# Spiking feed-forward layer: first layer over gathered w1 rows, and an idle add moved ahead of the second batch's tokens

## What is computed

```python
def _L0_cond_ref(inputs, initial_state):          # x (2, 2048, 512), cond (2, 512)
    rates = jax.nn.relu(inputs) * DT              # DT = 0.001
    c = initial_state[:, None, :] + jnp.cumsum(rates, axis=1)
    fl = jnp.floor(c)
    prev = jnp.concatenate([jnp.floor(initial_state)[:, None, :], fl[:, :-1, :]], axis=1)
    return (fl - prev) / DT

def _L0_ffn_ref(x, w1, b1, w2, b2):               # w1 (512, 2048), w2 (2048, 512)
    h = jax.nn.relu(jnp.einsum('bsd,dw->bsw', x, w1) + b1)
    return jnp.einsum('bsw,wd->bsd', h, w2) + b2

x = x + _L0_ffn_ref(_L0_cond_ref(x, cond), w1, b1, w2, b2)
```

## Time and profile before

| | |
|---|---|
| three runs | 108.17, 106.98, 107.22 us; median 107.22 |
| the profiled execution | 108.13 us, of which the span is 106.4 |
| busy in the span | TensorE 94.6 us (89%), VectorE 67.9, ScalarE 36.2, GpSimd 36.6 |
| data moved | 31.66 MB, mean 298 GB/s |
| mean granted clock of TensorE | 0.98 |

### The profile page before, as it was taken

One profiled execution on the slowest core, in us unless ns is written; L12 is line 12 of the kernel. 1 busy time (PEld: TensorE's weight loads), 2 busy tenths in 40 slices (PEclk: granted clock), 3 DMA queues, 4 the chain that ended last, 5 costly groups with the idle time before them and its releaser, 6 DMA issues.

```text
span 106.4 us, 1159 instructions
## 1 busy us (share of the span) xinstructions
PE 94.6 (89%) x375; PEld 52.2 (49%) x375; DVE 67.9 (64%) x137; ACT 36.2 (34%) x66; POOL 36.6 (34%) x41
## 2 busy tenths in 40 slices
PE   5999999999999999999895999999999999995000
PEld 5844444444644444634251444599999644441000
DVE  2348999888599999385445599999998700022000
ACT  2867515514382353189740000059443200000000
POOL 6200000000077500038300199960018780088720
PEclk9999999999999999999999999999999999999965
DMA  2999999999999999999992000499999999947850
GB/s 90 276 351 407 421 419 411 405 410 411 407 408 408 395 391 413 398 390 386 374 367 91 0 0 6 197 441 397 434 404 397 391 202 354 242 93 99 103 108 9
DMA packets 10028, 31.66 MB, mean 298 GB/s; under 512 B 1671, under 2 KB 1799, under 8 KB 8994
## 3 DMA queue, kind: packets, MB, share of 16 engines
q1 hardware_dynamic: 8304, 29.63, 72.4%
q0 software_dynamic: 1568, 1.90, 10.9%
q10 hardware_dynamic: 146, 0.01, 0.1%
HBM read 21.58 MB, written 10.75 MB: 304 GB/s over the span
## 4 chain that ended last, share of the span: by engine, by line
PE 43%; DVE 15%; POOL 13%; issue 12%; DMA 10%; POOLq 2%; DVEq 0%
PE ps_table L833 37%; DVE x_sb L697 8%; POOL out L357 8%; DMA rates<-in_x_turned,sixteen_at 5%; DMA out<-x_sb 5%; DVE spk_t L638 4%; PE ps_small L934 4%; POOL rates L352 3%; PE ps_turn L870 2%; POOLq L55 2%; POOL out L387 1%; POOL general_x L376 1%; DVE under L579 1%; DVE blocks_under L582 1%; POOLq L267 0%
## 5 line engine op out<-in xcount | busy, mean ns | idle before, releaser
L833 PE MATMUL ps_table<-w_sb 128*128 128x512 f32 x128 | 57.5, 602 | 0.1
L833 PEld LDWEIGHTS ps_table<-w_sb 128*128 128x128 f32 x128 | 24.0, 193 | 27.0 <-issue 26.2
L352 POOL DMA_INDIRECT rates<-in_x_turned,sixteen_at x8 | 9.6, 1198 | 36.9 <-DVE sixteen_at L583 35.0
L428 ACT ACTIVATE w_sb<-w_sb,b_col 128x512 f32<-128x512 f32 (+2 forms) x19 | 12.2, 642 | 16.7 <-DMA w_sb<-in_w_pairs 16.7
L357 POOL DMA_INDIRECT out<-w_sb,to_single x8 | 12.5, 1561 | 15.7 <-DMA out<-x_sb 13.8
L569 DVE SCALAR_TENSOR_TENSOR total_two<-x_sb,total_two 128x1024 f32<-128x1024 f32 x14 | 17.1, 1224 | 1.1 <-DMA x_sb<-in_x 0.6
L929 PE MATMUL ps_table<-w_sb 128*128 128x512 f32 x32 | 14.0, 595 | 0.0
L697 DVE TENSOR_TENSOR x_sb<-x_sb,ps_idle 128x2048 f32<-128x2048 f32 x6 | 13.4, 2277 | 0.1
L364 POOL TENSOR_TENSOR x_sb<-x_sb,idle_row 128x512 f32<-128x512 f32 x8 | 10.1, 1289 | 9.1 <-DVEq L738 9.1
L429 ACT ACTIVATE w_sb<-w_sb,minus_relu_b 128x512 f32<-128x512 f32 (+2 forms) x19 | 12.3, 649 | 0.6
L929 PEld LDWEIGHTS ps_table<-w_sb 128*128 128x128 f32 x32 | 6.0, 190 | 7.2 <-issue 6.9
(11 more groups left out here) (124 smaller groups left out, 54.2 us busy)
## 6 DMA issues: line engine op xcount, KB each, us to landing
x_sb<-in_x SPq DMA_DIRECT2D x16, 512.0 KB, 14.3
out<-x_sb SPq DMA_DIRECT2D x8, 1024.0 KB, 4.8
w_sb<-in_w_pairs SPq DMA_DIRECT2D x15, 512.0 KB, 15.5
w_sb<-in_w SPq DMA_DIRECT2D x4, 1024.0 KB, 16.0
w_sb<-in_w_pairs SPq DMA_DIRECT2D x2, 256.0 KB, 3.1
b_row<-in_b SPq DMA_DIRECT2D x1, 256.0 KB, 15.6
rates<-in_x_turned,sixteen_at POOLq DMA_INDIRECT x8, 5.9
out<-w_sb,to_single POOLq DMA_INDIRECT x8, 6.6
```

The costliest lines, as they stand in the source:

```text
L352: pool.indirect_dma_start(out=rates[:, col, :], out_offset=None, in_=x_sixteen, in_offset=bass.IndirectOffsetOnAxis(ap=sixteen_at[:, col:c ...
L428: chain(act.activation(weights, weights, ACT.Relu, bias=b1_col[:, m:m + 1], scale=PER_DT))
L833: last = pe.matmul(ps_table[c][:, :], table_hidden[:, m, c * P:(c + 1) * P], w2_sb[:, m, :], start=(m == 0), stop=(m == FC - 1))
```

## The change

The first layer of the general tokens no longer multiplies all 512 channels of `spk_t`. Each batch numbers its channels that have a slot (its members), at most 128: `count_members` and `place_members` give each member a place, a product with `place_hot` (`sum_places`) puts the members' channel, slot and row into places, `list_places` turns them into indices, and GpSimd gathers w1's rows for the places (`get_w1`, one indirect DMA of up to 128 rows of 8 KB for a batch). The first layer then is two products of 128 places by 128 slots for a chunk (`general_first`), and it alternates with the second layer (`general_second`). The four loads of `w1_sb` are gone from SyncE's queue (one is left in the redo branch).

The order changes with it. VectorE: `add_idle(0, 0, 4)` stands behind `place_members(0)` and ahead of `find_tokens(1)`; `list_general` stands ahead of the other idle adds; `list_singles` stands ahead of the fourth. TensorE: the new small products stand between parts of the table, `sum_rows` (now two products) between chunks 14 and 15, and the first layer waits for `general_listed` and both gathers. GpSimd: the two w1 gathers, then a wait for `general_listed` and the gather of `general_x`, then the two idle pieces; the wait for `adding` is gone. ScalarE copies the table's rows one step earlier. Memory for flags and facts, the numbering checks and two small conversions at the start change too; they are cut below.

```diff
-            for i in range(WQ):
-                part = slice(i * (F // WQ), (i + 1) * (F // WQ))
-                sp.dma_start(w1_sb[:, :, part], w1.rearrange("(c p) f -> p c f", p=P)[:, :, part]).then_inc(w1_in[i], 16)
...
-            for b in range(B):
+            def get_sixteens(b):
...
+            def get_w1(b):
+                pool.wait_ge(places_listed, b + 1)
+                pool.indirect_dma_start(out=w1_got_rows[b], out_offset=None, in_=w1,
+                                        in_offset=bass.IndirectOffsetOnAxis(ap=w1_at[b][:, :], axis=0)
+                                        ).then_inc(w1_got[b], 16)
...
+            get_sixteens(0)
+            get_sixteens(1)
+            get_w1(0)
             pool.wait_ge(idle_copied, 1)
-            pool.wait_ge(adding, 1)
+            get_w1(1)
+            pool.wait_ge(general_listed, 1)
+            pool.indirect_dma_start(out=general_x[:, :], out_offset=None, in_=x_rows,
+                                    in_offset=bass.IndirectOffsetOnAxis(ap=from_general[:, :], axis=0)
+                                    ).then_inc(general_got, 16)
             add_idle(1, 12, 16)
             add_idle(1, 8, 12)
             pool.wait_ge(singles_listed, 1)
             for b in range(B):
-                if b == 1:
-                    pool.wait_ge(general_listed, 1)
-                    pool.indirect_dma_start(out=general_x[:, :], out_offset=None, in_=x_rows,
-                                            in_offset=bass.IndirectOffsetOnAxis(ap=from_general[:, :], axis=0)
-                                            ).then_inc(general_got, 16)
...
+            act.wait_ge(table_summed, FC)
+            act.activation(table_row[0], ps_table[0][:, :], ACT.Copy).then_inc(table_rows_ready, 1)
             for m in range(FC):
                 relu_hidden(m, hidden_summed, m + 1, hidden_ready)
-                if 1 <= m <= DC:
-                    act.activation(table_row[m - 1], ps_table[m - 1][:, :], ACT.Copy).then_inc(table_rows_ready, 1)
+                if 1 <= m < DC:
+                    act.activation(table_row[m], ps_table[m][:, :], ACT.Copy).then_inc(table_rows_ready, 1)
...
+                chain(dve.tensor_scalar(facts_high[:, own(b), 2:3].rearrange("p e o -> p (e o)"), blocks_under[:, own(b)],
+                                        float(BLK), float(b * S), ALU.mult, ALU.add))
...
-                chain(dve.tensor_reduce(slot[:, mine], slot_part[:, :, :], AXIS.X, ALU.add))
-
-            def first_spikes():
-                chain(dve.tensor_tensor(spk_t[:, :, :], over(slot[:, own(0)], P), along(slot_name, DC), ALU.is_equal))
-
-            def second_spikes():
-                for c in range(DC):
-                    last = dve.scalar_tensor_tensor(out=spk_t[:, c, :], in0=slot_name, scalar=slot[:, DC + c:DC + c + 1],
-                                                    in1=spk_t[:, c, :], op0=ALU.is_equal, op1=ALU.add)
-                    if c < DC - 1:
...
-                last.then_inc(spk_ready, 1)
+                with nc.allow_low_precision(reason="whole numbers that the type holds"):
+                    chain(dve.tensor_reduce(facts_high[:, mine, 1:2].rearrange("p e o -> p (e o)"), slot_part[:, :, :],
+                                            AXIS.X, ALU.add))
+
+            def count_members(b):
+
+                mine = own(b)
+                chain(dve.tensor_scalar(is_member[:, mine], facts_high[:, mine, 1:2].rearrange("p e o -> p (e o)"), 0.5, None,
+                                        ALU.is_gt))
+                chain(dve.tensor_tensor_scan(member_run[b][:, :], ones[:, 0:DC], is_member[:, mine], 0.0, ALU.mult, ALU.add))
+                dve.sem_inc(members_counted, 1)
+                with nc.allow_low_precision(reason="whole numbers that the type holds"):
+                    chain(dve.tensor_reduce(facts_low[:, mine, 2:3].rearrange("p e o -> p (e o)"),
+                                            token_under[:, mine, 1:BLK], AXIS.X, ALU.add))
+
+            def place_members(b):
+                mine = own(b)
+                dve.wait_ge(members_before, b + 1)
+                chain(dve.scalar_tensor_tensor(out=place[:, mine], in0=member_run[b][:, :], scalar=ps_members[b],
+                                               in1=is_member[:, mine], op0=ALU.add, op1=ALU.mult))
+                chain(dve.tensor_tensor(place_hot[b][:, :, :], over(place[:, mine], P), along(slot_name, DC), ALU.is_equal))
+                dve.sem_inc(places_ready, 1)
+
+            def list_places(b):
+                dve.wait_ge(places_summed, b + 1)
+                dve.tensor_copy(w1_at[b][:, :], ps_places[b][:, 0:1]).then_inc(places_listed, 1)
+                dve.tensor_copy(place_fact[b][:, 1:2], ps_places[b][:, 2:3])
+                dve.tensor_scalar(place_slot[b][:, :], slot_name, ps_places[b][:, 1:2], None, ALU.is_equal).then_inc(
+                    slots_placed, 1)
...
-                chain(dve.tensor_reduce(tokens_under[:, :], token_under[:, :, 1:BLK], AXIS.X, ALU.add))
-                chain(dve.scalar_tensor_tensor(out=row_at[:, :], in0=blocks_under[:, :], scalar=float(BLK),
-                                               in1=tokens_under[:, :], op0=ALU.mult, op1=ALU.add))
+                chain(dve.tensor_tensor(row_at[:, :], facts_high[:, :, 2:3].rearrange("p e o -> p (e o)"),
+                                        facts_low[:, :, 2:3].rearrange("p e o -> p (e o)"), ALU.add))
                 chain(dve.tensor_scalar(not_single[:, :], met[:, :], 1.0, FAR, ALU.not_equal, ALU.mult))
...
+                for b in range(B):
+                    chain(dve.tensor_copy(checks[:, b + 1:b + 2], member_run[b][:, DC - 1:DC]))
...
-                chain(dve.tensor_scalar(slot_place[:, :], ps_rows[:, 1:3], slot_count[:, 0:1], None, ALU.mult))
+                chain(dve.tensor_scalar(slot_row[:, :], ps_rows[:, 1:2], slot_count[:, 0:1], None, ALU.mult))
                 chain(dve.tensor_scalar(none_far[:, :], ps_rows[:, 0:1], 0.5, FAR, ALU.is_lt, ALU.mult))
-                chain(dve.scalar_tensor_tensor(out=slot_row[:, :], in0=slot_place[:, 0:1], scalar=float(BLK),
-                                               in1=slot_place[:, 1:2], op0=ALU.mult, op1=ALU.add))
...
             find_sums(1)
             number_general(0)
             find_slots(0)
-            first_spikes()
+            count_members(0)
+            place_members(0)
+            add_idle(0, 0, 4)
             find_tokens(1)
+            list_places(0)
             find_general(1)
             number_general(1)
             find_slots(1)
-            second_spikes()
-            dve.sem_inc(adding, 1)
-            add_idle(0, 0, 4)
+            count_members(1)
+            place_members(1)
+            list_places(1)
+            list_general()
             add_idle(0, 4, 8)
             add_idle(0, 8, 12)
+            list_singles()
             add_idle(0, 12, 16)
-            list_singles()
-            find_members()
-            add_idle(1, 0, 4)
             find_odd()
             count_crowd()
-            list_general()
+            add_idle(1, 0, 4)
             add_idle(1, 4, 8)
...
+            def count_members(b):
+                pe.wait_ge(members_counted, b + 1)
+                pe.wait_ge(sums_ready, B)
+                pe.matmul(ps_members[b], upper_b[:, :], member_run[b][:, DC - 1:DC], start=True, stop=True).then_inc(
+                    members_before, 1)
+
+            def sum_places(b):
+                pe.wait_ge(places_ready, b + 1)
+                for facts in (facts_high, facts_low):
+                    for c in range(DC):
+                        last = pe.matmul(ps_places[b], place_hot[b][:, c, :], facts[:, b * DC + c, :],
+                                         start=(facts is facts_high and c == 0), stop=(facts is facts_low and c == DC - 1))
+                last.then_inc(places_summed, 1)
+
             def sum_rows():
-                pe.wait_ge(members_ready, 1)
-                for e in range(NE):
-                    last = pe.matmul(ps_rows, member[e // DC][:, e % DC, :], facts[:, e, :], start=(e == 0), stop=(e == NE - 1))
+                pe.wait_ge(slots_placed, B)
+                for b in range(B):
+                    last = pe.matmul(ps_rows, place_slot[b][:, :], place_fact[b][:, :], start=(b == 0), stop=(b == B - 1))
                 last.then_inc(rows_summed, 1)
+
+            def general_first(m):
+                if m >= 2:
+                    pe.wait_ge(hidden_ready, m - 1)
+                for b in range(B):
+                    last = pe.matmul(ps_hidden[m % 2][:, 0:P], w1_got_rows[b][:, m * P:(m + 1) * P], place_slot[b][:, :],
+                                     start=(b == 0), stop=(b == B - 1))
+                last.then_inc(hidden_summed, 1)
+
+            def general_second(m):
+                if m == 0:
+                    pe.wait_ge(table_rows_ready, 1)
+                pe.wait_ge(hidden_ready, m + 1)
```

(38 more changed lines are left out.)

68 lines of the change are left out of this document (37 added, 31 removed).

## The result

The changed kernel takes 115.22 us (114.21 to 115.37, four runs) against 107.55 in the runs beside it: 1.069 times as long, 95% interval 1.062 to 1.077. The direction was forecast, the size was not: 7.7 us more and not 2.8, outside the range. The profiled execution took 114.21 (span 112.4), the fastest of its kernel.

The account below looks back on a forecast made before the run. The landing of batch 1's last store (T), then GpSimd's scatters, bound the kernel, not TensorE. T moves from 92.9 to 95.7, 2.8 us later: 107.22 + 2.8 = 110.0 us, range 109.0 to 111.2.

Parts of the forecast that it names:

- What bounds the kernel: The end follows batch 1's last store and GpSimd's scatters; TensorE has 2.6 us to spare, its 7 us gain worth nothing.
- The add ahead of the tokens: VectorE's first idle add delays find_tokens(1) by 1.9 us; count_tokens(1) starts at 59.75 after TensorE idles 2.5 us.
- list_general ahead of the adds: VectorE waits some 3.3 us for sum_rows behind TensorE's chunk 14; list_general ends at 69.8.
- The adds and stores behind it: VectorE's remaining adds, list_singles (1.2 us) and checks (1.4) after list_general; adds end at 72.0, 74.2, 77.6, 81.2 and 83.4.
- T: Time at which batch 1's last store has landed: 95.7, from 78.3 + 12.3 + 4.8, 2.8 us later than 92.9.
- the small-share rival: Scatters get a small DMA share, some half of that work falls behind T: T about 93.2, 107.5 us; chance 0.10.
- The clock rival: TensorE's clock falls in the 2.5 us stall, chunk 14 takes 3.5 us more: 113.5 us; chance 0.06.
- The w1 gathers: GpSimd's gathers of w1 rows land in 4.0 to 8.4 us and cost nothing at the finish.

Follow-up runs that it names:

- e5: The changed kernel with all of list_singles in VectorE's wait for sum_rows and the checks behind the last idle add: 108.44 us, ratio 1.013 to the kernel before.
- e1: The changed kernel with only the row_at step moved into VectorE's wait for sum_rows: 114.96 us, ratio 1.070 to the kernel before.
- e3: e1 with find_odd and count_crowd behind the last idle add and TensorE's sum of the checks at chunk 13: 114.45 us, ratio 1.064.
- e4: The changed kernel with row_at, in its place, made from two contiguous float32 copies: 115.03 us, single run.
- p_stt: The changed kernel with row_at as a scalar_tensor_tensor: 114.87 us, single run.
- p_shift: Two probes: the changed kernel with the reduction met done twice (115.25 us) or three times (114.09 us, single run).
- p_gather_last: The changed kernel with GpSimd's gather of general_x behind its idle adds instead of ahead of them: 112.32 us, ratio 1.042 to the kernel before.
- e2: The changed kernel with each of GpSimd's eight idle adds waiting for the end of the one ahead: 110.77 us, single run.
- p_gather_ahead: The kernel before with GpSimd's idle adds released ahead of find_slots(1) and an unused gather directly ahead of them: 114.30 us, single run.
- e11: e5 with parts of chunk 13 ahead of count_tokens(1) and small products between parts of chunk 14 on TensorE: 104.84 us, ratio 0.976 to the kernel before.
- e6: e5 with the first idle add behind list_places(1) and list_singles, in VectorE's wait for sum_rows: 105.47 us, ratio 0.981 to the kernel before.
- e8: e6 with the sums only copied from PSUM, GpSimd's adds started earlier, list_general and the general_x gather later: 105.97 us, ratio 0.987 to the kernel before.

## Why the prediction was wrong

- **What bounds the kernel**: right. After the change, too, the end follows the last store of batch 1 and GpSimd's scatters, and TensorE's shorter first layer is worth nothing at the end of it.
- **The add ahead of the tokens**: right. `count_tokens(1)` at 59.84 (59.75 predicted) after 2.30 us of stall (2.5).
- **list_general ahead of the adds**: right. 3.46 us of idling (3.3), done at 69.91 (69.8).
- **"The adds and stores behind it"**: here the step failed. "`list_singles` with two steps less (1.2)" took 7.1 us, 74.22 to 81.34. The price came from the kernel before, where list_singles runs after GpSimd's adds; the change puts it beside them, and behind a gather. This term was sized as work and was a wait. Everything that I reckoned behind it (77.6, 81.2, 83.4) came about 6 us late. The checks, which I put at nothing, came late with it: TensorE waited 3.40 us for them and was done at 99.2 and not near 94, which cost nothing at the end.
- **T**: predicted from the store of (0,3), the arithmetic holds: that store was issued at 83.65 in the changed kernel, 83.65 + 0.7 + 12.3 + 4.8 gives 101.45. GpSimd's first scatter of batch 1 started at 100.33, so by the 0.3 us between the two in the kernel before T was near 100.0: the DMA sum was 1.4 us too dear, part of the way to the small-share rival. T came 4.3 us later than the 95.7 forecast, 6 from its late start less this; 110.0 + 4.3 is 114.3, 0.9 under the 115.22 measured. From 100.33 to the end of the span are 12.1 us; I had taken the 13.2 of the kernel before.
- **Without the held steps** (e5) the kernel takes 108.44 us, in the range, 1.6 under the forecast. It isn't quite the course that I reckoned with: list_singles (1.2 us) and the checks (1.4) are off the path there, and the low clock is on it, so that the closeness is in part luck.
- **The clock rival**: it was there, but smaller and elsewhere. In e1, with the same order as the changed kernel up to that point, the clock was at 0.50 from 62 to 64 us, and `list_places(1)` started at 66.04 and not at 64.97: 1.1 us, over before chunk 14. In the profiled execution of the change the clock stayed full there; its other runs have a mean clock of 0.917 to 0.930 against 0.941 and take 0.8 to 1.2 us more. That this is the same mechanism is likely but not seen in a trace of theirs. Of the profiled executions with this order and this stall, eight show the low clock behind it (e1, e3, e4, e5, p_stt, both p_shift and p_gather_last) and two, the change and e2, don't.
- **The w1 gathers** landed in 6.3 us (4.0 to 8.4 predicted) and cost nothing.

The sign that I passed over stands in the earlier trace rows: four steps of 128x128 in 4.18 us, beside one of 128x512 in 0.69. I used the first number as a date, and didn't ask why a step of a quarter of the size took longer.

"SBUF — State Buffer" of the Trainium skill (the section Who interferes with whom) says that a VectorE step with two SBUF inputs contends with a GpSimd step that reads SBUF, that a step in a mode which uses both of VectorE's port pairs contends with GpSimd too, and that a reduction, or a step with at most one SBUF input outside those modes, doesn't. The traces agree on which steps are held: row_at (two SBUF inputs) is; not_single (one) is, though no run here shows in which mode it works; `count_part` (one operand in PSUM), `met` (a reduction) and the idle adds (one operand in PSUM) beside the same run take 0.28, 0.29 and 2.28 as elsewhere. The section has the loser wait until the instruction that came first is done; behind a gather the measurement says otherwise: row_at stood through five GpSimd instructions, the first step of p_gather_ahead through all eight.

## What to carry to other kernels

A step's price holds for the neighbours it was measured beside: when a step moves, look at what runs on the other engines at its new place, and read a tiny step with a long duration as a wait. Steps of VectorE on SBUF operands go into its idle time or beside a GpSimd that is silent, and a GpSimd run that must stand beside them starts out of a wait in which GpSimd idles, not directly behind a gather. A wait that an in-order engine gets from another engine's order (here TensorE's chunk ahead of a small product) is worth filling before one blames the work that was moved: e11 keeps the moved add and is at least as fast as e6, which doesn't.

## What the runs showed of the hardware that was not expected

- GpSimd adds issued directly behind an indirect DMA held a VectorE step on SBUF operands for the rest of their run: 5.54 to 6.19 us of 9.84 in the changed kernel's variants, in p_gather_ahead 10.54 us for the first of four steps, through the rest of the gather and all 9.81 us of the run. The same adds started out of a wait let one in at each boundary: 1.16 and 1.19 us in p_gather_last, 1.35 each for the spk_t steps.
- A tensor_scalar of 128x8 with a single float32 operand in SBUF is held like a step with two (6.19 us in e1). Steps of one column with one tensor operand were not held, although the run stood directly behind a gather (e8: 0.14 to 0.21 us within GpSimd's last add, from 73.36 to 74.62). One column alone is no way out: the addition of two SBUF columns in e2 took 1.11 us, to the end of a GpSimd add:

```profile
80.80 1.11 DVE L703 TENSOR_TENSOR checks<-many_run 128x1 f32<-128x1 bf16 x1
```

- After a stall of 2.3 us the clock of TensorE went to its lower level (0.50) for some 3 us in eight profiled executions, e1 and e5 among them, and stayed at 1.00 in those of the changed kernel and e2, with the same stall.
